# Order of the gather rows and the count words in the preparation of a graph-network kernel

## The chip, the cores and the metric

The kernel runs on one core of a Trainium2 chip. The metric is the device time of one execution in microseconds (us). A core has TensorE (PE; PEld is its weight load), VectorE (DVE), ScalarE (ACT), GpSimd (POOL) and SyncE (SP), which issues most transfers; GpSimd issues the indirect fetches.

## The reference, cut to what matters

The inputs are 12500 nodes with 64 features (`x`), 400000 edges (`src`, `dst`, sorted by `dst`) and 64 attributes for each edge. Three rounds each gather the features of every edge's source node and add them up at its destination:

```python
edge_index = jnp.stack([src, dst])
x = _layernorm(x + _L0_gnn_ref(x, src, dst, L0_gnn_W_fc, L0_gnn_b_fc, L0_gnn_W_res, L0_gnn_b_res), axis=-1)
x = _layernorm(x + _L1_gnn_ref(x, edge_index, edge_attr_64, ...), axis=-1)
# inside: segment_sum(x[src], dst) in L0; segment_sum(x[src] @ Wm + edge_attr @ We, dst) twice in L1
```

## The kernel before, in words

The sums over edges are done in two ways. Most edges are **counted**: for a window of 1, 2 or 4 destination nodes, a matmul of two one-hot matrices counts how many edges come from each source node, and the counts (kept as an adjacency matrix) are multiplied with the features. Edges that no window covers are **gathered**: their source rows are fetched from a table in memory and added with a one-hot matmul. Both ways need codes for every edge, and all codes depend on the data, so the program makes them itself. This is the **preparation**, the first stage of the program; nothing of the main loops starts before the step marked `prepared` (L730). The change touches preparation alone.

The edges form T = 3125 tiles of 128. There are 34 columns (CG) of 128 count steps, so CW = 4352 columns, and 26 columns (SG) of 128 gather steps, SPAD = 3328. The order of the work on each engine is written out by hand; engines meet at semaphores. VectorE numbers most of its instructions on one semaphore (`step`), and other engines wait for a named mark in that count.

VectorE in order: it finds where windows lie among the tiles (`c_tile`, L552); marks the covered edges and packs source, destination and that mark into one word for each edge (`both`, L571), which SP stores to `both_dram` (L1479); counts listed tiles (`sums`, L582). Then, as the kernel stands:

- **Count list** (L585 to L594): GpSimd has fetched 34 columns of `dst` tile rows into `rows_ct` (L1233, L1234); VectorE compares and counts in two halves (L587, L589) and writes the indices `c_idx`.
- **Gather list** (L597 to L649): after two small products of TensorE (L1030, L1031) VectorE finds the tile and the block of every gather step and writes `g_idx` (L646).
- **Edge list and path** (L652 to L665), then two memsets and two instructions on all count columns (L671, L672).
- **x loop** (L674 to L685): with TensorE (L1058) and ScalarE (L1343, L1346) the table of the first round, y, is made in 7 iterations of 14 blocks and stored by SP (L1494).
- **Unpacking of the count words** (L687 to L699): 16 instructions on 4352 columns (two of the steps are four instructions each, one for each window width, `spans_of`), after all 34 fetches into `rows_c` have landed. The codes lie in `accf` (`rel`) and `tmp_c`.
- **Unpacking of the gather rows** (L703 to L714): 6 instructions for each half of 13 columns, when that half of the fetches has landed. They write `src_g` and `rel_g`.
- Two sums of biases, then 14 **copies of the turned gather codes** from PSUM (L724), a wait, and the memset `prepared` (L730).

GpSimd issues the fetches in this order: 34 for `rows_ct`; 34 of count words (`c_idx`, L1237); 26 of gather rows (`g_idx`, L1239, L1240). Then three memsets: most of `abuf[:, 1]` (L1242) after the x loop, the accumulator (L1245) after the marks of L714 and ScalarE's turned codes, and the rest of `abuf[:, 1]` (L1247) after VectorE's copies. All fetches stand on one line, that of the helper `fetch` (L1228).

TensorE turns the codes by transposes of 128 columns, four to a PSUM bank: `prepare` (L1012) for those that ScalarE copies out (L1337, one instruction for each 128 columns; count codes are written twice side by side), `prepare_side` (L1021) for those that VectorE copies out. SP loads x in 14 transfers (L1490) after `c_idx`.

## Time and profile before

| | us |
|---|---|
| median of 3 runs | 3540.97 (3540.76 to 3543.51) |
| the profiled execution | 3540.19 |
| its span, first to last instruction | 3538.4 |
| preparation, until `prepared` | 258.3 |
| busy in the span: PE, DVE, POOL, ACT | 3093.2, 2386.6, 2122.3, 1585.2 |

How to read it: a timeline row gives the start in us from the span's start, the duration, the engine, the line of the kernel, the operation, the tiles written and read with partitions x elements, how many instructions are merged (x5), and in brackets how long the engine sat idle before and what released it. The stage table gives busy time and, in brackets, the number of instructions in each window; PEclk is the granted TensorE clock as a share of full speed. A landing is the time from the start of a DMA's issue until its data are there. Preparation is one chain through several engines: a busy share alone says little there, and what counts is who waits for whom.

### The profile page before, as it was taken

How to read it: one execution, taken by the hardware profiler on the slowest of the kernel's cores; microseconds unless marked ns; L12 is line 12 of the kernel's file. 1: busy time of each engine (PE TensorE's matmuls, PEld its weight loads, DVE VectorE, ACT ScalarE, POOL GpSimd, SP SyncE). 2: the span in 40 equal slices, each digit the busy share in tenths (PEclk: the TensorE clock that was granted, in tenths of full speed). 3: DMA queues.
4: the chain of work that ended last, by engine and by line, in shares of the span. 5: the costliest groups of instructions: out<-in, count | busy, mean ns of one | idle time of the engine just before them, and what ended most of it. 6: DMA issues, size and time to landing. Idle time of an engine off the chain costs nothing.

```text
span 3538.4 us, 114817 instructions
## 1 busy us (share of the span) xinstructions
PE 3093.2 (87%) x38568; PEld 2873.9 (81%) x38568; DVE 2386.6 (67%) x6286; ACT 1585.2 (45%) x2164; POOL 2122.3 (60%) x2436
## 2 busy tenths in 40 slices
PE   0228999999999999889999979999999889999995
PEld 0127988888888888778888879999999789999995
DVE  8679998988888888689999673333333433333335
ACT  0122677778999999689999550000000400000000
POOL 5771345455666666444444257777777777777774
PEclk9869999999999999999999879999999999999998
DMA  3521455555666666578888439999999499999995
GB/s 86 145 18 44 162 200 203 201 219 223 242 242 242 242 242 242 216 225 253 253 252 253 131 117 386 393 396 383 400 391 385 176 358 398 387 388 398 383 394 222
DMA packets 234014, 928.09 MB, mean 262 GB/s; under 512 B 46723, under 2 KB 146193, under 8 KB 178030
## 3 DMA queue, kind: packets, MB, share of 16 engines
q1 hardware_dynamic: 182559, 846.33, 63.9%
q0 software_dynamic: 51392, 80.97, 8.0%
q8 instruction: 34, 0.56, 0.1%
q14 instruction: 29, 0.24, 0.0%
HBM read 676.56 MB, written 250.56 MB: 262 GB/s over the span
## 4 chain that ended last, share of the span: by engine, by line
PE 40%; POOL 18%; issue 17%; DVE 13%; DMA 6%; DVEq 5%; ACT 1%; ACTq 0%; POOLq 0%; SPq 0%
PE ps L1124 28%; POOL msg L1286 13%; PE ps L1147 8%; DVE union L815 5%; DMA msg<-y_tab,idx 4%; POOL abuf L1228 3%; DVE union L929 3%; PE ps L1116 3%; DVE abuf L942 2%; DVEq L942 2%; DVEq L470 2%; POOL union L1228 1%; PE ps L1084 1%; DMA abuf<-in_x_dram 1%; PE ps L1203 1%
## 5 line engine op out<-in xcount | busy, mean ns | idle before, releaser
L1286 POOL DMA_INDIRECT msg<-y_tab,idx x1512 | 1612.8, 1067 | 920.1 <-issue 469.3
L1124 PE MATMUL ps<-union,abuf 128*128 128x192 bf16 x14112 | 1205.8, 248 | 15.9 <-DVEq L786 10.2
L1124 PEld LDWEIGHTS ps<-union,abuf 128*128 128x128 f16 x14112 | 1173.2, 99 | 18.9 <-issue 10.6
L1416 ACT ACTIVATE abuf<-ps 128x784 f16<-128x784 f32 x1152 | 949.1, 824 | 261.7 <-PE ps L1147 236.9
L815 DVE TENSOR_TENSOR union<-lane,union 128x1568 f16<-128x1568 f16 (+1 forms) x1384 | 912.2, 711 | 8.2 <-PE ps L1147 4.9
L1124 PE MATMUL ps<-early,abuf 128*128 128x195 bf16 x7154 | 809.3, 249 | 0.0
L1124 PEld LDWEIGHTS ps<-early,abuf 128*128 128x128 f16 x7154 | 641.9, 99 | 92.1
L1147 PE MATMUL ps<-union 128*128 128x98 f16 (+2 forms) x4192 | 661.3, 287 | 56.9 <-DVE union L815 55.9
L1392 ACT ACTIVATE idx<-src_g 128x7 int32 (+1 forms) x216 | 44.4, 206 | 1255.8 <-PE ps L1116 1228.1
L807 DVE TENSOR_TENSOR acc<-acc,ps 128x64 f32 (+1 forms) x1015 | 225.3, 222 | 409.4 <-DVE acc L807 239.6
L1194 PE MATMUL ps<-union 128*64 128x128 f32 x7280 | 458.5, 278 | 24.2 <-ACT union L1434 19.6
L1194 PEld LDWEIGHTS ps<-union 128*64 128x64 f32 x7280 | 395.4, 137 | 87.5 <-DVE abuf L942 75.6
L1434 ACT ACTIVATE union<-union 128x1280 f32<-128x1280 f16 x364 | 443.6, 1268 | 35.7 <-DVE union L929 35.3
L1147 PEld LDWEIGHTS ps<-union 128*128 128x128 f16 x4192 | 353.2, 108 | 98.5 <-issue 58.8
L1306 POOL TENSOR_TENSOR rel_e<-early,base_e 128x10 f16 x728 | 225.7, 329 | 261.1 <-DVE union L929 244.8
L929 DVE TENSOR_TENSOR union<-lane,rel_e 128x640 f16<-128x640 f16 x728 | 353.6, 486 | 4.4 <-POOL rel_e L1306 1.4
L890 DVE TENSOR_REDUCE part_d<-ps 128x64 f32<-128x192 f32 x144 | 51.6, 359 | 356.9 <-PE ps L1124 356.9
L793 DVE TENSOR_SCALAR hot_g<-lane,codes 128x128 f16<-128x128 f16 x1008 | 182.4, 272 | 63.6 <-DVE acc L807 62.1
L1116 PE MATMUL ps<-msg,hot_g 128*128 128x64 bf16 (+1 forms) x4536 | 182.2, 195 | 43.5 <-DMA msg<-y_tab,idx 43.2
L942 DVE TENSOR_TENSOR abuf<-abuf,ps 128x128 f32 x728 | 206.2, 283 | 15.4 <-issue 7.2
L1116 PEld LDWEIGHTS ps<-msg,hot_g 128*128 128x128 f16 x4536 | 169.4, 99 | 52.9 <-DMA msg<-y_tab,idx 52.0
L864 DVE TENSOR_TENSOR acc<-acc,ps 128x65 f32 x504 | 110.6, 219 | 69.0 <-DVE acc L864 53.8
(231 smaller groups left out, 1342.2 us busy)
## 6 DMA issues: line engine op xcount, KB each, us to landing
abuf<-a_dram SPq DMA_DIRECT2D x288, 1568.0 KB
a_dram<-abuf SPq DMA_DIRECT2D x72, 3136.0 KB
union<-in_edge_attr_dram SPq DMA_DIRECT2D x728, 160.0 KB, 3.1
msg<-y_tab,idx POOLq DMA_INDIRECT x1512
y_tab<-union SPq DMA_DIRECT2D x28, 336.0 KB, 2.2
abuf<-in_x_dram SPq DMA_DIRECT2D x28, 224.0 KB, 3.7
y_tab<-early SPq DMA_DIRECT2D x7, 682.5 KB, 5.6
out_dram<-union SPq DMA_DIRECT2D x2, 800.0 KB, 3.5
```

The costliest lines, as they stand in the source:

```text
L807: V.tensor_tensor(to, to, tile_ps(r, j, k).unsqueeze(1), ALU.add).then_inc(s_add[r], 1)
L815: return V.tensor_tensor(to.rearrange("p s (c u) -> p s c u", u=2), lanes.unsqueeze(1).to_broadcast([P, n, width // 2, 2]), codes[:, which ...
L929: marks = V.tensor_tensor(mark_e[:, h, :, :].rearrange("p j (c u) -> p j c u", u=2), lane16[:, 0:P].rearrange("p (c u) -> p c u", u=2).uns ...
L942: V.tensor_tensor(to, to, ps[:, b, 0:P], ALU.add).then_inc(e_add, 1)
L1116: last = nc.tensor.matmul(tile_ps(r, j, k), hot_g[:, s, :], msg[:, s, c * width_of[r]:(c + 1) * width_of[r]], start=c == 0, stop=c == 2)
L1124: last = nc.tensor.matmul(ps[:, bank, 0:3 * width_of[r]], abuf[:, buffer, hi * P:(hi + 1) * P], ycols[r][:, hi, :], start=hi == 0, stop=hi ...
L1147: nc.tensor.matmul(ps[:, w % 4, 0:WIN].rearrange("p (h d) -> p h d", d=WD)[:, :, d0:d0 + wd], hot_c[:, n, WIN:WIN + P], hot_c[:, n, 0:HIS ...
L1194: last = nc.tensor.matmul(ps[half:half + D, h, 0:P], feats[:, h, j * D:(j + 1) * D], hot_e[:, h, j, :], start=j < 2, stop=j >= EG - 2)
L1286: pool.indirect_dma_start(msg[:, s, 0:3 * width_of[r]], None, y_tab[r], bass.IndirectOffsetOnAxis(ap=idx[:, s:s + 1], axis=0)).then_inc(ga ...
L1306: nc.gpsimd.tensor_tensor(rel_e[:, h, :, :], flat(dst_e[:, bass.ds(grp[h], 1), :]).unsqueeze(2) .to_broadcast([P, EG, 2]), base_e[:, bass. ...
L1416: A.activation(abuf[:, j, :].rearrange("p (h w d) -> p w h d", w=WPB, d=WD) [:, w:w + 2, :, :], ps[:, w % 4:w % 4 + 2, 0:WIN].rearrange("p ...
L1434: A.activation(hot_e[:, h:h + 2, :, :], mark_e[:, h:h + 2, :, :], ACT.Copy)\
```

## The change

The gather list moves ahead of the count list on VectorE, and the fetches of gather rows ahead of those of the count words on GpSimd. The first half of the gather rows is unpacked before the x loop, the second after it. The count words are fetched and unpacked in two halves, 16 and 18 columns (`C_HALF` = 16). ScalarE copies out the gather codes and the first half of the count codes, and of the second half the one table (`twice_h`); VectorE copies the other (`twice_l`), 5 groups. ScalarE now copies a whole group of 512 columns by one instruction. `rel` moves from `accf` to a part of `abuf` (`rel_cf`), and the memsets change accordingly. Cut to its core (the function `unpack_g` holds the six instructions of L706 to L714 as they were; of the count list and the unpacking of count words, moved or cut to column ranges, only the heads stand here):

```diff
+    C_HALF = BC // 2 * 4
+    BL = BC - BC // 2
+    BP = 1 + 2 * BG + 2 * BC - BL
...
+        rel_cf = af[:, 2 * SPAD:2 * SPAD + CW]
...
             step(V.tensor_tensor_scan(upto[:, 0:TC], node[:, 0:TC], spans[:, 0:TC], 0.0, ALU.mult, ALU.add), "sums")
-            for c0, c1, landed in ((0, CG // 2, s_g[2]), (CG // 2, CG, s_late)):
...
-            step(V.tensor_copy(gidx[:, 2, :], small[:, 18, :]), "c_idx")
...
             step(V.scalar_tensor_tensor(base_n, blk_n, float(P), past_n, ALU.mult, ALU.add))
+            for c0, c1, landed in ((0, CG // 2, s_g[2]), (CG // 2, CG, s_late)):
...
+            step(V.tensor_copy(gidx[:, 2, :], small[:, 18, :]), "c_idx")
...
-            rel, tmp = accf[:, 0:CW], tmp_c
+            rel, tmp = rel_cf, tmp_c
...
+            unpack_g(0, SG // 2, s_g[0])
             for i in range(XITER + 1):
...
-            dve.wait_ge(s_g[1], 16 * CG)
...
+            unpack_g(SG // 2, SG, s_last)
+            for c0, c1, landed, upto, name in ((0, C_HALF, s_g[1], 16 * C_HALF, "code_0"),
+                                               (C_HALF, CG, s_late, 16 * (CG - CG // 2 + CG - C_HALF), "code_1")):
+                dve.wait_ge(landed, upto)
...
-            for to, first in ((code_g, 0), (src_g, BG)):
-                for n in range(first, first + BG):
-                    dve.wait_ge(s_ptd, n + 1)
-                    g0 = (n - first) * 4
-                    width = min(4, SG - g0) * P
-                    V.tensor_copy(to[:, g0 * P:g0 * P + width], ps[:, 4 + n % 4, 0:width]).then_inc(s_pd, 1)
-            dve.wait_ge(s_pd, 2 * BG)
+            for n in range(BL):
+                dve.wait_ge(s_ptd, n + 1)
+                cols = slice(C_HALF * P + n * 4 * P, min(C_HALF * P + (n + 1) * 4 * P, CW))
+                width = cols.stop - cols.start
+                V.tensor_copy(twice_l[:, cols, :], ps[:, 4 + n % 4, 0:width].unsqueeze(2).to_broadcast([P, width, 2]))\
+                    .then_inc(s_pd, 1)
+            dve.wait_ge(s_pd, BL)
+            dve.wait_ge(s_pc, BP)
...
-            prepare(0, 1 + BC)
...
+            prepare(0, BP - BL)
+            pe.wait_ge(x_left, XITER)
+            for n in range(BL):
+                prepare(BP - BL + n, BP - BL + n + 1)
+                prepare_side(n)
...
-            pool.wait_ge(s_v, mark["c_idx"])
+            pool.wait_ge(s_v, mark["g_idx"])
             pool.wait_ge(s_both, 32)
-            fetch(rows_c, single(both_dram), 2, range(CG), s_g[1])
-            pool.wait_ge(s_v, mark["g_idx"])
             fetch(rows_g, tiles_of(both_dram), 0, range(SG // 2), s_g[0])
             fetch(rows_g, tiles_of(both_dram), 0, range(SG // 2, SG), s_last)
-            LEFT = 2 * (2 * SPAD) - HIS * P
+            pool.wait_ge(s_v, mark["c_idx"])
+            fetch(rows_c, single(both_dram), 2, range(C_HALF), s_g[1])
+            fetch(rows_c, single(both_dram), 2, range(C_HALF, CG), s_late)
+            LEFT, RIGHT = 2 * (2 * SPAD) - HIS * P, 2 * (2 * SPAD + CW) - HIS * P
             pool.wait_ge(x_low, XITER)
-            pool.memset(abuf[:, 1, LEFT:], 0.0).then_inc(s_clear, 1)
-            pool.wait_ge(s_pc, 1 + BC)
-            pool.wait_ge(s_v, mark["src_g"])
+            pool.memset(abuf[:, 1, RIGHT:], 0.0).then_inc(s_clear, 1)
+            pool.wait_ge(s_pc, 1 + 2 * BG)
+            pool.memset(abuf[:, 1, 0:LEFT], 0.0).then_inc(s_clear, 1)
+            pool.wait_ge(s_v, mark["rel_g"])
             pool.memset(acc_all[:, :, :], 0.0).then_inc(s_clear, 1)
-            pool.wait_ge(s_pd, 2 * BG)
-            pool.memset(abuf[:, 1, 0:LEFT], 0.0).then_inc(s_clear, 1)
...
+                    elif jobs[n][2] is not None:
+                        to = jobs[n][2]
+                        frm = ps[:, n % 4, 0:to.shape[1]]
+                        if len(to.shape) == 3:
+                            frm = frm.unsqueeze(2).to_broadcast(list(to.shape))
+                        last = A.activation(to, frm, ACT.Copy)
```

## Rows read from the trace of the kernel before

**Rows 1.** Stages: window, length, busy us of PE, PEld, DVE, ACT, POOL, PEclk

```profile
0.00:258.50 258.50, 38.48 (x289) 35.56 (x289) 195.35 (x208) 33.72 (x86) 176.15 (x109) 0.83 0.39 85
...
142.20:160.20 18.00, 10.50 (x71) 9.78 (x71) 14.94 (x15) 11.24 (x15) 14.10 (x13) 0.83 0.86 279
...
167.30:204.50 37.20, 0.02 (x1) 0.03 (x1) 36.55 (x16) 0.00 (x0) 33.84 (x12) 0.50 0.27 30
...
207.20:215.30 8.10, 5.49 (x35) 4.17 (x33) 7.89 (x6) 8.10 (x32) 7.34 (x3) 0.91 0.30 30
```

**Rows 2.** Timeline of GpSimd: start, duration, line, operation, idle time before it

```profile
114.31 0.94 POOL L1228 DMA_INDIRECT union<-both_dram,gidx  x1 [8.04 <-DVE tiles L598]
...
138.54 4.51 POOL L1228 DMA_INDIRECT union<-both_dram,gidx  x1 [0.30 <-issue]
...
199.92 4.62 POOL L1228 DMA_INDIRECT abuf<-both_dram,gidx  x1 [0.31 <-issue]
...
224.44 0.94 POOL L1228 DMA_INDIRECT abuf<-both_dram,gidx  x1 [0.30 <-issue]
...
225.37 9.94 POOL L1242 MEMSET abuf<- 128x11776 f16 x1
...
239.29 6.39 POOL L1245 MEMSET acc<- 128x6500 f32 x1 [3.99 <-DVE abuf L709]
```

**Rows 3.** Timeline of VectorE in preparation, same columns

```profile
108.26 2.42 DVE L587 TENSOR_TENSOR abuf<-abuf,sc 128x2176 f32<-128x2176 int32 x1 [12.84 <-DMA abuf<-in_dst_dram,gidx]
...
114.07 0.16 DVE L598 COPY tiles<-ps 125x1 f32<-125x1 f32 x1
...
131.32 0.18 DVE L646 CAST gidx<-small 128x26 int32<-128x26 f32 x1
...
137.55 4.69 DVE L672 TENSOR_TENSOR union<-lanef,small 128x4352 f32<-128x4352 f32 x1
...
167.36 2.43 DVE L688 TENSOR_SCALAR union<-union 128x4352 int32<-128x4352 int32 x1 [7.22 <-DMA union<-both_dram,gidx]
...
202.00 2.43 DVE L699 CAST union<-union 128x4352 f32<-128x4352 int32 x1
...
214.25 1.03 DVE L714 TENSOR_SCALAR abuf<-abuf 128x1664 f32<-128x1664 f32 x1
...
231.37 4.82 DVE L706 TENSOR_SCALAR acc<-abuf 128x1664 int32<-128x1664 int32 x1 [16.09 <-DMA abuf<-both_dram,gidx]
...
242.20 4.37 DVE L714 TENSOR_SCALAR abuf<-abuf 128x1664 f32<-128x1664 f32 x1
...
247.84 1.48 DVE L724 CAST code_g<-ps 128x512 f16<-128x512 f32 x2 [0.50 <-PE ps L1021]
...
250.05 2.93 DVE L724 CAST code_g<-ps 128x512 f16<-128x512 f32 x5 [0.73 <-PE ps L1021]
...
258.27 0.17 DVE L730 MEMSET part_d<- 128x130 f32 x1 [0.99 <-POOL abuf L1247]
```

**Rows 4.** Groups of instructions: GpSimd's gather-row fetches (165 to 225.5 us)

```profile
L1228 POOL DMA_INDIRECT abuf<-both_dram,gidx x26 | 52.5, 2019 | 7.9 <-issue 7.9
```

**Rows 5.** Timelines of TensorE and ScalarE in preparation, same columns

```profile
91.01 0.57 PE L1031 MATMUL ps<-tiles,hot_g 125*128 125x1 f32 x2
...
246.62 1.97 PE L1021 MATMUL ps<-ident,abuf 128*128 128x128 f32 x8 [31.26 <-DVE abuf L714]
...
250.92 5.48 ACT L1337 ACTIVATE union<-ps 128x256 f16<-128x256 f32 x18 [0.23 <-PE ps L1012]
```

**Rows 6.** DMA issues: median us from issue to landing (125 to 140; 224 to 226 us)

```profile
union<-both_dram,gidx POOLq DMA_INDIRECT x12, 2.6
...
abuf<-both_dram,gidx POOLq DMA_INDIRECT x2, 6.8
```

**Rows 7.** Stage table, first steps of the main loop (columns as in rows 1)

```profile
262.00:266.00 4.00, 3.73 (x23) 3.35 (x24) 3.41 (x7) 0.00 (x0) 3.14 (x3) 0.50 0.20 37
...
280.00:290.00 10.00, 8.47 (x90) 6.87 (x88) 10.00 (x20) 1.65 (x2) 0.00 (x0) 1.00 0.01 2
```

More of the change, by code:

```diff
@@ L649, in _ @@
             step(V.scalar_tensor_tensor(base_n, blk_n, float(P), past_n, ALU.mult, ALU.add))
+            for c0, c1, landed in ((0, CG // 2, s_g[2]), (CG // 2, CG, s_late)):
+                dve.wait_ge(landed, 16 * (c1 - c0))
+                step(V.tensor_tensor(by_step(before_ct)[:, c0:c1, :], by_step(rows_ct)[:, c0:c1, :],
+                                     over(sc[:, 0, c0:c1], c1 - c0), ALU.is_lt))
+                step(V.tensor_reduce(small[:, 16, c0:c1], by_step(before_ct)[:, c0:c1, :], AX.X, ALU.add))
+            step(V.scalar_tensor_tensor(small[:, 17, :], small[:, 6, :], float(P), small[:, 16, :],
+                                        ALU.mult, ALU.add))
+            step(V.tensor_tensor(small[:, 17, :], small[:, 17, :], sc[:, 1, :], ALU.add))
+            step(V.tensor_scalar(small[:, 18, :], small[:, 17, :], float(E - P), None, ALU.min))
+            step(V.tensor_copy(gidx[:, 2, :], small[:, 18, :]), "c_idx")
             e_left, e_grp, e_blk, e_base, e_hit = (small[:, k, 0:ES] for k in (2, 3, 4, 5, 12))
@@ L673, in _, with unpack_g @@
                                  over(small[:, 3, :], CG), ALU.is_lt))
+            lane_bits = P.bit_length() - 1
+            def unpack_g(c0, c1, landed):
+                dve.wait_ge(landed, 16 * (c1 - c0))
+                n, cols = c1 - c0, slice(c0 * P, c1 * P)
+                step(V.tensor_single_scalar(lane_of[:, 0:n * P], rows_g[:, cols], P - 1, op=ALU.bitwise_and))
+                step(V.tensor_scalar(block_of[:, cols], rows_g[:, cols], lane_bits, P - 1,
+                                     ALU.logical_shift_right, ALU.bitwise_and))
+                step(V.scalar_tensor_tensor(src_gf[:, cols], lane_of[:, 0:n * P], float(BLOCKS), block_of[:, cols],
+                                            ALU.mult, ALU.add), "src_g")
+                step(V.tensor_single_scalar(rows_g[:, cols], rows_g[:, cols], BITS, op=ALU.logical_shift_right))
+                step(V.tensor_tensor(by_step(rel_gf[:, cols]), by_step(rows_g[:, cols]), over(base_n[:, c0:c1], n),
+                                     ALU.subtract))
+                step(V.tensor_scalar(rel_gf[:, cols], rel_gf[:, cols], -1.0, float(P), ALU.max, ALU.min), "rel_g")
+            unpack_g(0, SG // 2, s_g[0])
             for i in range(XITER + 1):
@@ L685, in _ @@
                                     yparts[0][:, x_blocks(i - 1), 1, 0:D], ALU.subtract).then_inc(x_low, 1)
-            dve.wait_ge(s_g[1], 16 * CG)
-            step(V.tensor_scalar(dst_c, rows_c, BITS, WIDE - 1, ALU.logical_shift_right, ALU.bitwise_and))
-            step(V.tensor_tensor(by_step(rel), by_step(dst_c), over(sc[:, 0, :], CG), ALU.subtract))
-            for s0, s1, wd in spans_of:
-                step(V.scalar_tensor_tensor(tmp[:, s0:s1], rel[:, s0:s1], float(wd), tmp[:, s0:s1], ALU.is_ge, ALU.add))
@@ L980, in _ @@
                         V.tensor_tensor(squares[:, blk, :], feat[:, blk, :], over_d(rstd[:, blk]), ALU.mult).then_inc(f_scaled, 1)
[L983 to L989 removed]
+        jobs = [(mark["path"], [(regs, 64, P, trT)], None)]
+        for into, frm, name, to, first, cols in ((jobs, rel_gf, "rel_g", code_g, 0, SG), (jobs, src_gf, "rel_g", src_g, 0, SG),
+                                                 (jobs, rel_cf, "code_0", twice_h, 0, C_HALF), (jobs, tmp_c, "code_0", twice_l, 0, C_HALF),
+                                                 (jobs, rel_cf, "code_1", twice_h, C_HALF, CG), (side_jobs, tmp_c, "code_1", twice_l, C_HALF, CG)):
+            for g0 in range(first, cols, 4):
+                g1 = min(g0 + 4, cols)
+                into.append((mark[name], [(frm[:, g * P:(g + 1) * P], P, P, None) for g in range(g0, g1)],
+                             to[:, g0 * P:g1 * P, ...]))
+        assert len(side_jobs) == BL and len(jobs) == BP
         e_src = dst_rows.rearrange("p (a q j) -> p a j q", a=TC // EG, j=EG)
@@ L1060, in _ @@
                 last.then_inc(x_prod, 1)
-            prepare(0, 1 + BC)
-            side = 0
-            for n in range(1 + BC, 1 + 2 * BC):
-                prepare(n, n + 1)
-                while side < 2 * BG and (side < 2 * (n - BC - 2) or n == 2 * BC):
-                    prepare_side(side)
-                    side += 1
+            prepare(0, BP - BL)
[3 more added lines that the diff above has]
+                prepare_side(n)
             for r in range(3):
```

65 lines of the change are left out of this document (20 added, 45 removed).

## The prediction, made before the changed kernel ran

> **What bounds the kernel now.** I read the stage table first, because every edit lies before the first product of the main loops. Preparation ends at 258.5 us, and VectorE is busy for 195 of them, GpSimd for 176 [rows 1]. The chain of waits then names GpSimd's gather fetches for most of this stage, so I followed VectorE's and GpSimd's timelines side by side. The reader is to see three things in them.
>
> First, GpSimd has one queue of 94 fetches, about 1.24 us apart when nothing is in their way (0.94 plus 0.30 of issue), and the last ends at 225.38 [rows 2]. It stands idle for 8.04 us between 106.26 and 114.31, while VectorE in turn waits 12.84 us for the last rows of the second search [rows 2, 3].
>
> Second, the fetches lengthen beside certain VectorE work. The 26 gather-row fetches take 52.5 us of execution plus 7.9 of issue, against 32.2 at the free pace [rows 4]. One lasts 4.51 us and ends 0.81 after L672, which reads two SBUF tensors, has ended (142.24); another lasts 4.62, past the start of L699's cast (202.00), and ends 0.11 after that has ended (204.43) [rows 2, 3]. So a fetch that meets a two-input instruction must wait for its end to begin, and beside the doubled-rate single-input ones it is held a second time before it can finish. Beside the unpacking of the count words (167.36 to 204.43) twelve fetches fill a stretch of 37.2 us [rows 1]; 14.9 would do.
>
> The Trainium skill ("SBUF — State Buffer", the section on the shared port pair) infers that a tensor_tensor leaves descriptor generation alone. The L672 row disagrees: 4.51 against 0.94. I follow the row; the rule is a rival below.
>
> Third, a GpSimd memset does the reverse: VectorE's L706 takes 4.82 us and L714 4.37, against 1.03 for another L714 of the same size, and both end 0.9 us after a memset does [rows 2, 3]. Behind the last landing come the unpacking of the second half of gather rows, TensorE's turning of them, 14 VectorE copies, and the reset that lets all engines go at 258.27 [rows 3].
>
> **The change part by part.**
>
> *The gather list goes first.* The list needs TensorE's two small products (91.58) [rows 5] and then 17.4 us of VectorE (114.07 to 131.50) [rows 3]: it is ready at 109.1. GpSimd's search fetches lose the company of one two-input instruction of 2.42 us (about 1.6 us less) and gain that of the list's (about 3): they end near 107.7. GpSimd's idle time falls from 8.04 to some 1.7, and the first gather fetch starts at 109.4. The count list now comes behind: four instructions of 2.42 and four small ones put it at 120.5, 6.6 later than now, but its fetches wait for 26 others anyway. Queued behind the same mark on SP are 14 loads of x, also 6.6 later; VectorE wants the products of the first only at 144, so that costs nothing; if the loads took all of the 23 us from 120.5, it would still be covered.
>
> *26 gather fetches.* 32.2 us free. What they meet: the two L587 (about 1.6 and 1.2 lost), L672 (3.4), the unpacking of their own first half (about 3.5), and a stretch of the x loop (1.2). Together 10.9, so GpSimd is done with them at 152.5. The first 13 are issued by 131.4. They land 2.6 to 6.8 us after their start, by the fast and the slow row [rows 6]; I take 136, since the loads of x run beside. VectorE is then held at that wait from 130.5, with the x loop queued behind it: 8.1 us of unpacking to 144, 18.0 of x loop to 162, 8.1 for the other half to 170 [rows 1]. The next thing for VectorE comes only at 181.7, so up to 11 us of delay here is covered.
>
> *16 count fetches.* 19.8 free, about 3.3 lost to the x loop and 4.6 to the second unpacking (as the three fetches beside that work lose now): issued by 180.1, landed by 181.7.
>
> *First half of the count words.* The 16 instructions now take 37.1 us. With 0.195 us of each fixed (0.16 from the two sizes 1.03 at 1664 and 2.43 at 4352 columns, and the gap) there are 33.9 us by size. 2048 of 4352 columns in 14 instructions cost 16.0 + 2.7 = 18.7: 181.8 to 200.5.
>
> *18 count fetches beside it.* Free 22.3. The loss is the term the trace doesn't show. Bounds: nothing, or the 0.60 us per us that the full-size instructions cost now (22.3 over 37.2), 11.2 over 18.7. Walking the fetches past the shorter instructions by the two rules above lets eight through in the stretch and loses 9.4; I take that, near the upper end because the same kinds of instruction stand there. The queue ends at 211.8; the last fetch starts at 210.9 and, landing like the lone count fetches (2.6), is in at 213.5.
>
> *Memsets.* GpSimd goes straight from the last fetch to its first memset, 3072 columns, 2.6 us at L1242's rate [rows 2], to 214.5. VectorE's first instruction of the second half is a doubled-rate one and waits for that: 0.9 lost (between nothing and the 9.6 of all three memsets: 11776 columns take 9.94 now, the accumulator's 6.39). The 6.4 us memset of the accumulator should follow beside two-input instructions, which do not wait for a memset now.
>
> *Second half of the count words.* 2304 columns in 12 instructions: 18.0 + 2.3 = 20.3, to 234.8. This used to be hidden behind the gather fetches; now the gather rows are hidden and this lies on the path.
>
> *The tail.* The 14 VectorE copies of gather codes (about 0.6 each, 8.4 us) go to ScalarE between 170 and 181, where it is idle now: nothing. Left are ten groups, five on each engine. VectorE's first copy stands 1.27 us after the unpacking now; one group of four transposes comes ahead of it, about 1.0 (eight take 1.97) [rows 3, 5]. Four copies of 1.14 (0.59 plus 512 more elements at 1.08 ns, L672's rate) and a short one of 0.65 make 5.2. With 0.15 until the reset: 7.6 us. ScalarE's five, at four times 0.304 each [rows 5], end by 6.8. The reset comes at 242.4 instead of 258.27.
>
> *Sum.* The queue's end moves by 13.6 us (8.04 - 1.7 = 6.3 of idle time, 7.3 of less holding), the way from there by 2.3 (32.9 to 30.6): 15.9. The profiled execution took 3540.19 with a span of 3538.4, 0.78 under the median, so 3524.3 on its scale and **3525.0** as a median. All later stages are unchanged and only begin earlier. A measurement of this kernel can tell about 0.2%, 7 us, from no change.
>
> **The rivals.**
>
> *Late landing meets the memset* (0.17). The last lone gather fetches land 6.8 us after their start, not 2.6 [rows 6]. If the last count fetches do so, the data come at 217.7, in the middle of the accumulator's memset (215.1 to 221.5), and the first instruction waits as L714 does now. From 221.5: 20.4 and 7.6 give 249.5, a gain of 8.8: 3532. Against it: twelve count fetches in a row landed in 2.6. It decides if the data come after 215.1.
>
> *Little holding* (0.10). If the fetches slip through between the halved instructions, up to 9.4 us more are won: 3516 to 3520.
>
> *Two-input instructions hold no fetch* (0.03). Then the gather and count fetches lose only what five doubled-rate instructions per half cost, the queue ends near 191, and the reset comes near 221: 3504. The 4.51 us row speaks against it. This is what the Trainium skill's inference (same page and section) would make of it.
>
> *The clock of the first steps* (0.03), the slower side. TensorE starts the main loop at the lower of its two levels (1.2 GHz): 0.50 from 262 to 266 with 23 products in 4 us; later it is at 1.00 with 90 in 10 [rows 7]. It has fewer transposes to do just ahead. Each us at the low level loses 1 - 5.75/9.0 = 0.36 us; the gain is gone after 44 us of it, and twice that would cost 32: 3557. Against it: it starts low now as well, and the whole of preparation has work for TensorE in 38 of 258 us either way [rows 1].
>
> *The reset is not what the main loop waits for, or the lists do not come early* (0.05): 3541. Nothing in the trace supports it: VectorE waits for nothing but the last memset there, and the main loop's first instructions follow the reset [rows 3].
>
> **How the numbers follow.** The forecast has 0.62, with its own range of 3520 to 3530 (holding 5 to 11.2, landing 2.4 to 4). The range reaches over the late landing and part of the little holding: 3517 to 3533. Faster by over 0.2% (below 3533.9): 0.62 + 0.17 + 0.10 + 0.03, less 0.03 for a worse mix, 0.89; within: 0.07; slower: 0.04.
>
> **What would show it.** The first gather fetch near 109.4; fetch 26 ending near 152.5; first-half gather wait on VectorE until about 136; an idle stretch on VectorE from 170 to 182; about eight fetches between 182 and 200; the last issue near 212; the first instruction of the second half lengthened by under 1 us; the reset near 242. It is wrong if the queue ends outside 204 to 215, or if the step from the last landing to the reset is not near 29 us.

## The result, and the profile after

The change made the kernel slower, by a third of a per cent. In eight runs of each the kernel before took 3541.44 us (median; 3539.79 to 3543.63) and the changed kernel 3552.64 us (3550.02 to 3555.53): a ratio of 1.0033, 95% interval 1.0024 to 1.0042. The forecast was 3525.0 us with a range of 3517 to 3533. The profiled execution of the changed kernel took 3550.02 us with a span of 3548.3, so it compares with the profiled 3540.19 (span 3538.4) of before.

Preparation did win. The time came back more than a thousand microseconds later, in two stages that the change doesn't touch: the **edge loop** (VectorE marks edges one-hot, TensorE multiplies, VectorE adds the products up; 728 steps, 32 to a turn of VectorE's loop) and the **fold** behind it (196 fp32 products of 128 x 64 columns). From the starts of four rows in each trace (the resetting memset, the loop's first marks, the fold's first product and the end):

| stretch | before, us | after, us | difference |
|---|---|---|---|
| start to `prepared` | 258.27 | 246.35 | -11.9 |
| `prepared` to the edge loop's first marks | 1252.71 | 1251.86 | -0.9 |
| edge loop, first marks to fold | 478.68 | 482.76 | +4.1 |
| fold | 22.10 | 40.60 | +18.5 |
| end of the fold to the end of the span | 1526.64 | 1526.73 | +0.1 |

The resets and the folds stand further down and in [rows 3]; the first marks, of before and of after:

```profile
1510.98 0.49 DVE L929 TENSOR_TENSOR union<-lane,rel_e 128x640 f16<-128x640 f16 x1 [1.40 <-POOL rel_e L1306]
```

```profile
1498.21 0.49 DVE L940 TENSOR_TENSOR union<-lane,rel_e 128x640 f16<-128x640 f16 x1 [1.40 <-POOL rel_e L1317]
```

**Preparation.** The stage table of the changed kernel, columns as in [rows 1]: all of preparation, the x loop, the unpacking of the first half of the count words, and the first steps of the main loop.

```profile
0.00:246.50 246.50, 42.12 (x289) 39.89 (x289) 193.55 (x209) 33.25 (x45) 158.05 (x109) 0.83 0.41 89
148.00:171.50 23.50, 12.35 (x71) 11.41 (x71) 14.73 (x14) 11.23 (x15) 18.12 (x18) 0.72 0.93 209
179.60:198.30 18.70, 7.91 (x52) 7.67 (x52) 18.23 (x14) 6.97 (x14) 16.26 (x9) 0.68 0.31 49
...
250.00:254.00 4.00, 3.65 (x22) 3.27 (x23) 3.40 (x7) 0.00 (x0) 3.08 (x4) 0.50 0.18 37
```

VectorE's work is nearly the same, GpSimd's is 18 us less; the x loop takes 23.5 us instead of 18.0, for the same work [rows 1]. The main loop starts at the same low clock, with one product fewer in 4 us [rows 7]. The timeline of GpSimd, columns as in [rows 2]:

```profile
109.44 0.94 POOL L1239 DMA_INDIRECT abuf<-both_dram,gidx  x1 [2.27 <-DVE small L639]
...
127.11 4.51 POOL L1239 DMA_INDIRECT abuf<-both_dram,gidx  x1 [0.31 <-issue]
...
150.90 1.14 POOL L1239 DMA_INDIRECT abuf<-both_dram,gidx  x1 [0.30 <-issue]
...
208.68 0.94 POOL L1239 DMA_INDIRECT union<-both_dram,gidx  x1 [0.30 <-issue]
209.62 2.68 POOL L1254 MEMSET abuf<- 128x3072 f16 x1
212.22 0.76 POOL L1256 MEMSET abuf<- 128x768 f16 x1
212.89 5.53 POOL L1258 MEMSET acc<- 128x6500 f32 x1
```

These are the first, the 13th and the 26th gather fetch, the last count fetch and the three memsets behind it. The idle time ahead of the first gather fetch has shrunk from 8.04 to 2.27 us, and the queue ends at 209.62 instead of 225.38 [rows 2]. The same on VectorE, columns as in [rows 3]:

```profile
126.11 4.69 DVE L676 TENSOR_TENSOR union<-lanef,small 128x4352 f32<-128x4352 f32 x1
139.92 1.03 DVE L684 TENSOR_SCALAR acc<-abuf 128x1664 int32<-128x1664 int32 x1 [9.11 <-DMA abuf<-both_dram,gidx]
...
168.39 1.09 DVE L700 TENSOR_TENSOR abuf<-ps,early 128x896 f32<-128x896 f32 x1 [6.03 <-ACT early L1357]
...
179.61 1.23 DVE L713 TENSOR_SCALAR union<-union 128x2048 int32<-128x2048 int32 x1
...
211.60 8.04 DVE L713 TENSOR_SCALAR union<-union 128x2304 int32<-128x2304 int32 x1 [13.32 <-DMA union<-both_dram,gidx]
219.68 2.56 DVE L714 TENSOR_TENSOR abuf<-union,sc 128x2304 f32<-128x2304 int32 x1
...
237.21 1.36 DVE L724 CAST union<-union 128x2304 f32<-128x2304 int32 x1
...
246.35 0.17 DVE L741 MEMSET part_d<- 128x130 f32 x1
```

Two rows need a second look. L713 of the second half takes 8.04 us; another single-input instruction of the same size, the cast L724, takes 1.36. It ends at 219.64, which is 1.22 us after the last of GpSimd's three memsets has ended (212.89 + 5.53 = 218.42): it was kept out through all three. And the x loop stands still for 6.03 us at 162, because TensorE waits for x; this one is covered.

**Fold.** The timelines of TensorE, first of the kernel before and then of the changed one:

```profile
1981.92 6.47 PE L1194 MATMUL ps<-union 128*64 128x128 f32 x100 [0.34 <-DVE abuf L942]
1989.66 22.10 PE L1203 MATMUL ps<-twofold,abuf 128*128 128x64 f32 x196 [1.27 <-DVE abuf L953]
```

```profile
1973.23 6.48 PE L1205 MATMUL ps<-union 128*64 128x128 f32 x100 [0.38 <-DVE abuf L953]
1980.97 40.60 PE L1214 MATMUL ps<-twofold,abuf 128*128 128x64 f32 x196 [1.26 <-DVE abuf L964]
```

The stage tables of the fold tell why, again of before and then of after:

```profile
1990.00:1995.00 5.00, 5.00 (x47) 5.00 (x46) 0.69 (x1) 1.19 (x2) 0.00 (x0) 1.00 0.01 3
```

```profile
1980.00:1985.00 5.00, 4.03 (x26) 4.03 (x27) 1.57 (x4) 0.60 (x1) 0.00 (x0) 0.76 0.01 3
1985.00:1990.00 5.00, 5.00 (x25) 5.00 (x25) 0.00 (x0) 0.60 (x1) 0.00 (x0) 0.50 0.00 0
```

The granted clock is 1.00 (2.4 GHz) before and 0.50 (1.2 GHz) after: 47 products in 5 us against 25. A mean of 0.76 from 1980 to 1985 is 2.6 us at the full clock, so it falls at 1982.6, 1.6 us after the fold has begun. TensorE worked at the full clock until then but for a pause of 1.26 us in front of the fold, where it waits for VectorE's last additions. The kernel before has the same pause, 1.27 us, and keeps its clock.

**Edge loop.** Short waits of VectorE ahead of its additions, in the view of waits over the loop (line waited at, releaser, us in total, times, longest; "issue": nothing that the profile shows), of before and then of after:

```profile
DVE abuf L942 <- issue: 7.2, 25, 0.3
```

```profile
DVE abuf L953 <- issue: 14.5, 66, 0.4
```

In the timeline they come once per turn of the loop before and three times after. A turn takes 20.74 us before and 20.97 after:

```profile
1576.23 0.29 DVE L942 TENSOR_TENSOR abuf<-abuf,ps 128x128 f32 x1 [0.29 <-issue]
...
1596.97 0.29 DVE L942 TENSOR_TENSOR abuf<-abuf,ps 128x128 f32 x1 [0.29 <-issue]
```

```profile
1557.75 0.29 DVE L953 TENSOR_TENSOR abuf<-abuf,ps 128x128 f32 x1 [0.15 <-issue]
...
1563.28 0.29 DVE L953 TENSOR_TENSOR abuf<-abuf,ps 128x128 f32 x1 [0.29 <-issue]
...
1565.94 0.29 DVE L953 TENSOR_TENSOR abuf<-abuf,ps 128x128 f32 x1 [0.17 <-issue]
...
1578.72 0.29 DVE L953 TENSOR_TENSOR abuf<-abuf,ps 128x128 f32 x1 [0.15 <-issue]
```

### The profile page after: what moved, and what is told of

Its sections match the earlier page's. It is cut to its first block, busy times and chain, and to the rows that moved or that the text cites. A ratio compares the mean times of both kernels' runs of the same rounds, so it can differ in the third digit from the quotient of the medians.

```text
span 3548.3 us, 114777 instructions
## 1 busy us (share of the span) xinstructions
PE 3114.4 (88%) x38568; PEld 2894.7 (82%) x38568; DVE 2383.8 (67%) x6287; ACT 1584.4 (45%) x2123; POOL 2101.3 (59%) x2436
## 4 chain that ended last, share of the span: by engine, by line
PE 35%; issue 19%; POOL 17%; DVE 16%; DMA 6%; DVEq 5%; ACT 1%; POOLq 0%; SPq 0%; ACTq 0%
PE ps L1135 23%; POOL msg L1297 15%; PE ps L1158 7%; DVE union L826 5%; DMA msg<-y_tab,idx 4%; DVE union L940 3%; PE ps L1127 2%; DVE abuf L953 2%; DVEq L953 2%; DVEq L474 2%; PE ps L1214 1%; DMA abuf<-in_x_dram 1%; DVE union L570 1%; PE ps L1095 1%; POOL abuf L1281 0%
## 5 line engine op out<-in xcount | busy, mean ns | idle before, releaser
L953 DVE TENSOR_TENSOR abuf<-abuf,ps 128x128 f32 x728 | 204.8, 281 | 20.3 <-issue 14.5
```

The source lines that it names most:

```text
L953: V.tensor_tensor(to, to, ps[:, b, 0:P], ALU.add).then_inc(e_add, 1)
```

## The experiments

The first theory was that the loss hangs on *when* the edge loop runs (the shift; theory A of the first expectations, where theory B is that something else in the changed kernel holds the clock down). The second was that it hangs on *where* the loop lies in VectorE's program (the place). e1 to e8 are one execution each, beside one of the kernel before; the others are medians of 4 to 12. In two expectations (e6, e8) the change is said to add some ten VectorE instructions ahead of the loop; counted in the compiled programs it adds one (1120 before, 1121 after: the two sums of biases). Where a short wait count is given below, it is that of the additions from first marks to fold, as shown above; expectations that say 64 counted over a window a little shorter.

### Is it the shift? e1_pad12 and e2_pad2

```diff
+            for _ in range(7):
+                step(V.memset(hot_g[:, :, :], 0.0))
+            step(V.memset(hot_g[:, 0:10, :], 0.0))
             step(V.memset(part_d[:, :, :], 0.0), "prepared")
```

> The changed kernel with eight extra VectorE memsets (about 12 us) just ahead of the reset, which give back what preparation won and do nothing else. Theory A (the level of TensorE's clock in the fold hangs on when the fold begins, because the 1.3 us pause ahead of it can bring the lower level): the 196 fold products may return to about 22 us, and the time is then near 3546 (3552.6 + 12 - 18.5). Theory B (something the change left behind, not the shift, holds the clock low): the fold stays at 40.6 us and the time is near 3564.

3564.91 us, the reset at 254.08 (7.7 us later than in the changed kernel, not the 12 of the expectation), the fold still slow:

```profile
1993.14 39.74 PE L1217 MATMUL ps<-twofold,abuf 128*128 128x64 f32 x196 [1.26 <-DVE abuf L967]
```

e2 adds one full memset and one of three columns (1.9 us, two instructions).

> The changed kernel with about 1.9 us of extra VectorE memsets ahead of the reset. Theory A: the fold can come out either way, 22 or 40.6 us, with a time near 3536 or 3554.5; a 22 here would show that 2 us of shift are enough to change the clock. Theory B: 40.6 us, near 3554.5.

3553.38 us, the fold 40.34 us, 66 short waits. Two delays, and the fold slow at each: starting later gives nothing back. Both pads also add VectorE instructions ahead of the loop, eight and two; that this matters came out only with e5 and e6.

### Is it the pause ahead of the fold? e3_fill

```diff
+                    pe.wait_ge(e_add, ESTEPS + EB)
+                    for n in range(16):
+                        nc.tensor.matmul(ps[0:D, 0, 0:P], feats[:, 0, 0:D], hot_e[:, 0, 0, :], start=True, stop=True)
                     pe.wait_ge(e_add, ESTEPS + LAG + EB)
                     for n in range(FOLDS):
```

> The changed kernel with 16 dummy products of the edge loop's shape between the last edge product and the fold, written to a PSUM bank that the fold overwrites: TensorE's pause of 1.26 us goes, nothing else moves. Theory A (the pause brings the low level): granted clock 1.00 over the fold, fold 22 us, time near 3534. Theory B (the fold's products cannot hold the clock after this change whatever comes ahead): fold 40.6, time unchanged near 3552.6.

3541.55 us, 11 under the changed kernel; 3534 was forecast. Against the profiled execution of the changed kernel the edge loop with the added products took 2.8 us more, and the stretch behind the fold 6.4, which no run explains. TensorE's timeline has no pause in front of the fold, and the fold runs at the full clock:

```profile
1980.99 3.66 PE L1211 MATMUL ps<-union 128*64 128x128 f32 x32
1984.58 22.10 PE L1217 MATMUL ps<-twofold,abuf 128*128 128x64 f32 x196
```

The pause is needed for the fall. It doesn't bring it about alone, since the kernel before has it too. VectorE's short waits (62) stay as in the changed kernel, and the loop stays long (485.6 us with the added products in it).

### What did the memsets cost? e4_dve_memsets

The three memsets go to VectorE, into its idle time ahead of the second half of the count words; GpSimd's are removed.

```diff
+                if c0:
+                    dve.wait_ge(x_low, XITER)
+                    step(V.memset(acc_all[:, :, :], 0.0))
+                    step(V.memset(abuf[:, 1, RIGHT:], 0.0))
+                    dve.wait_ge(s_pc, 1 + 2 * BG)
+                    step(V.memset(abuf[:, 1, 0:LEFT], 0.0))
                 dve.wait_ge(landed, upto)
```

> The changed kernel with GpSimd's three memsets moved to VectorE, into its idle stretch ahead of the second half of the count words. If the memsets held VectorE's first instruction of that half (8.04 us against 1.36), it now takes 1.4 and the reset comes 5.5 to 6.7 us earlier, near 240; if that instruction was slow for another reason, it stays at 8 and nothing moves. The memsets may slow fetches beside them by up to 3 us. The total is not forecast beyond this: theory A lets the fold come out at 22 or 40.6, so 3527 or 3546; theory B says 3546.

3547.76 us. In VectorE's timeline the first instruction of the second half takes 1.36 us and the reset comes 6.7 us earlier; the fold took 40.16 us again.

```profile
199.34 5.47 DVE L713 MEMSET acc<- 128x6500 f32 x1 [1.42 <-issue]
...
211.28 1.36 DVE L720 TENSOR_SCALAR union<-union 128x2304 int32<-128x2304 int32 x1 [4.22 <-DMA union<-both_dram,gidx]
...
239.66 0.17 DVE L747 MEMSET part_d<- 128x130 f32 x1
```

So the held instruction cost what the row says, 8.04 - 1.36 = 6.7 us.

### Does the kernel before lose it too? e5_before_pad2, e6_before_tiny10, e15_before_tiny1, e10_before_gpsimd_pad

e5 is the kernel before with the two memsets of e2 ahead of the reset; e6 and e15 put ten and one memsets of a single element into an early wait of VectorE:

```diff
+            for _ in range(10):
+                step(V.memset(part_d[0:1, 0, 0:1], 0.0))
             dve.wait_ge(stored[0], 16)
```

> The kernel before with about 1.9 us of extra VectorE memsets ahead of the reset, nothing else. Theory A (the fold's clock hangs on where its pause falls in time, and the kernel before is lucky): the fold may fall to the low level, about 40 us instead of 22.1, and the time is then near 3561; if it stays at 22 the time is near 3543. Theory B (the changed preparation itself is the cause): 22 us and 3543 for certain.

> The kernel before with ten one-element memsets on VectorE early in preparation, where it waits for a load anyway: no step of preparation moves, but VectorE's later instructions lie ten places further on, as in the changed kernel. If the edge loop's extra waits of the changed kernel (64 short ones called issue against 25) come from where VectorE's instructions lie: about 64 waits and an edge loop (first marks to fold) 3 to 5 us longer than 478.7. If they come from anything else: 25 waits and 478.7. The fold comes out at 22 or 40 under theory A, at 22 under theory B.

e5 took 3565.90 us and e6 3567.86, against 3540.83 of the kernel before beside them. Nothing of the change is in either, and both show the whole loss. Of e5, the timeline of TensorE and the view of waits:

```profile
1995.92 39.68 PE L1206 MATMUL ps<-twofold,abuf 128*128 128x64 f32 x196 [1.26 <-DVE abuf L956]
```

```profile
DVE abuf L945 <- issue: 14.9, 68, 0.4
```

e6 speaks against the shift: its ten instructions lie in an idle wait, and its reset comes at 259.59, 1.3 us later than before.

e10 is the counterpart: the delay without a VectorE instruction, by three more memsets on GpSimd that VectorE's wait ahead of the reset includes.

```diff
+            pool.wait_ge(s_clear, 2)
+            for n in range(3):
+                pool.memset(abuf[:, 1, 0:LEFT], 0.0).then_inc(s_clear, 1)
+                pool.wait_ge(s_clear, 3 + n)
             pool.memset(abuf[:, 1, 0:LEFT], 0.0).then_inc(s_clear, 1)
```

> The kernel before with three further GpSimd memsets of 0.8 us each ahead of the resetting memset, each behind the last: the later stages begin some 2.4 us later, as in the padded kernel before with two instructions on VectorE, but VectorE's program has no instruction more. The place of the edge loop: 25 short waits, the edge loop 478.7 us, the fold 22.1 us, the program 3542 to 3545 us. The shift in time: the fold 40 us, the program 3560 to 3566 us.

3543.58 us (ratio 1.0009, 0.9993 to 1.0024), with one of ten executions at 3560.80. The reset comes at 261.38, later than in e5 and e6, and there are 25 short waits and a fast fold, as the place has it and the shift does not:

```profile
1991.16 22.10 PE L1203 MATMUL ps<-twofold,abuf 128*128 128x64 f32 x196 [1.24 <-DVE abuf L953]
```

> The kernel before with one one-element memset on VectorE in an early wait. A place that a single instruction reaches: 60 to 67 short waits, the edge loop 483 us, the fold 22 or 40 us, the program 3544 or 3562 us. A boundary that lies further (two instructions reached it in e5): 25 waits, 478.7 us, 3541 us.

3542.39 us (ratio 1.0002, 0.9987 to 1.0018), with one of ten executions at 3559.65; in the profile 25 short waits, the fold 22.10. One instruction more does nothing to the kernel before; two do.

### Is it chance? e7_after_again

The changed kernel, unaltered.

> The changed kernel once more, unaltered, for another trace. Theory A with a chance phase in every run: the fold comes out at 22 in some runs. If it is 40 again, with the clock falling at another distance from the pause, the outcome belongs to the program more than to chance. Time near 3552.6.

3555.64 us, the fold 40.58 us, 64 short waits: the same again.

### Undo the one instruction: e9_after_one_sum

```diff
-            for c in range(2):
-                step(V.tensor_tensor(bme[:, c, 0, :], bme[:, c, 0, :], bme[:, c, 1, :], ALU.add))
+            step(V.tensor_tensor(bme[:, :, 0, :], bme[:, :, 0, :], bme[:, :, 1, :], ALU.add))
```

> The changed kernel with its two sums of the biases written as one instruction over both codes, as in the kernel before: VectorE's program then has as many instructions ahead of the edge loop as before the change (the changed kernel has one more). Nothing else moves. The place of the edge loop in VectorE's program: the short waits of VectorE in the edge loop number about 25 as before (64 in the changed kernel), the edge loop from its first marks to the fold takes 478.7 us (482.8), the fold's 196 products take 22.1 us at the full clock (40.6), and the program takes 3541.4 - 11.9 = 3529.5 us (3526 to 3532). The rival, that the shift in time of the edge loop decides (it begins 12 us earlier than before): 62 to 67 waits or not, the fold takes 40 us and the program 3549 to 3556 us.

3529.74 us as a median of twelve, forecast 3529.5; ratio to before 0.9963 (0.9947 to 0.9978). The whole change of preparation is in it, and the reset comes at 247.77. The timeline of TensorE and the view of waits:

```profile
1977.88 22.10 PE L1213 MATMUL ps<-twofold,abuf 128*128 128x64 f32 x196 [1.26 <-DVE abuf L963]
```

```profile
DVE abuf L952 <- issue: 7.4, 26, 0.3
```

The edge loop takes 478.63 us, as before. One instruction decides over some 23 us (3552.64 - 3529.74). One of the twelve executions took 3547.06 us, 17 above the median, about the fold's price; it has no profile.

### A version that beats both, and what a place is: e8, e11 to e14, e16 to e18

e8 joins e3 and e4 and adds 54 one-element memsets, to move the loop on in VectorE's program.

> The changed kernel with the dummy products ahead of the fold, the three memsets on VectorE, and 54 one-element VectorE memsets early in preparation (where it waits for a load), which with the change's ten put VectorE's later instructions 64 places on. Dummy products: fold 22, so about 16 us less than 3552.6 (18.5 less 2.3 of their own). Memsets: about 6.5 less. Together 3530. If 64 places bring the edge loop back to 25 waits, another 4 less: 3526; if not, 3530.

3529.41 us, with a fast fold (the filling products) and an edge loop of 484.32 us, as long as ever: 46 waits at the additions and 21 at the marks. Moving on by 58 instructions did not bring the short loop back.

e11 goes the other way: e4 and e9 together, and three memsets of the start moved to GpSimd, so that VectorE has 1120 instructions ahead of the loop, as in the kernel before. e12 is e11 with e3's filling products.

```diff
-            V.memset(steps[0:1, 0:GW + SETS * GW + EDGE0], 0).then_inc(s_zero, 1)
-            V.memset(w_cat[:, :, :, :], 0.0).then_inc(s_zero, 1)
-            V.memset(w_y0[:, :, :], 0.0).then_inc(s_zero, 1)
...
+            pool.memset(w_cat[:, :, :, :], 0.0).then_inc(s_zero, 1)
+            pool.memset(w_y0[:, :, :], 0.0).then_inc(s_zero, 1)
+            pool.memset(steps[0:1, 0:GW + SETS * GW + EDGE0], 0).then_inc(s_zero, 1)
```

> The changed kernel with the three memsets on VectorE's idle stretch instead of GpSimd, the sums of the biases as one instruction, and three memsets of the start on GpSimd, so that VectorE's program again has as many instructions ahead of the edge loop as before the change. The place of the edge loop: 25 short waits, the edge loop 478.7 us, the fold 22.1 us, resetting memset at 240, the program 3541.4 - 11.9 - 6.6 = 3523 us (3519 to 3527). The shift in time: the fold 40 us, the program 3542 to 3548 us.

> The same with 16 products whose result nobody reads between the last edge product and the fold. The fold takes 22.1 us under both theories. The place of the edge loop: 25 short waits, the edge loop with the added products 481 us, the program 3523 + 2.4 = 3525.5 us (3521 to 3529), slower than without them by 2.4 us. The shift in time: 62 to 67 waits and an edge loop of 485 us, the program 3529 us, faster than without them by 15 us.

Neither theory had e11 right: 68 short waits in spite of the equal count, a loop of 482.63 us, and in the profiled execution a fast fold (3523.38 us). Its ten executions fall into two groups, four from 3523 to 3530 us and six from 3543 to 3552; the median of 3544.06 (ratio 0.9997, 0.9978 to 1.0015) lies in the upper one. That the groups are the fold at its two clocks is inferred from their distance, since no execution of the upper one was profiled. e12, where TensorE doesn't pause, has no such groups, though it is slower than both theories said (3525.5 and 3529): 3531.22 to 3533.66, median 3532.21, ratio 0.9968 (0.9954 to 0.9983).

e13 drops one of e11's waits that earlier instructions imply. The expectation counts it as a second semaphore of the accumulator's memset; in the built program it is an instruction of its own ahead of that memset. e14 is e13 with the filling products.

```diff
-                    dve.wait_ge(x_low, XITER)
                     step(V.memset(acc_all[:, :, :], 0.0))
```

> e11_best_plain without VectorE's wait on the x products ahead of the moved memsets, which its earlier copies imply: the same instructions, one instruction with two semaphores fewer. If a second semaphore takes a place in VectorE's program: some 25 short waits instead of 65, the edge loop 478.7 us instead of 482.6, the program 3519 to 3524 us wherever the fold runs at the full clock (22.1 us). If it takes none: 65 waits and an edge loop of 482.6 us as in e11.

> The same with 16 products whose result nobody reads between the last edge product and the fold. If a second semaphore takes a place: some 25 short waits, the edge loop from first marks to the fold 478.7 + 2.4 = 481.1 us, the fold 22.1 us in every run, the program 3532 (e12) - 4 = 3528 us. If it takes none: 65 waits and 3532 us as e12.

Both missed: 61 short waits, a loop of 482.94 us. e13 again falls into two groups (four of twelve at 3527 to 3528, eight from 3544 to 3549; median 3544.54, ratio 0.9994, 0.9976 to 1.0012), e14 does not (median 3530.57, ratio 0.9958, 0.9942 to 0.9974).

e16 and e17 then take one and two further instructions off VectorE's program ahead of the loop; e18 is e17 with the filling products.

```diff
-            step(V.memset(dsts[0:1, 0:HALO], -1000))
...
-            step(V.memset(ones_t, 1.0))
...
+            pool.memset(sums[0:TP, TP:TP + P], 1.0).then_inc(s_const, 1)
+            pool.memset(dsts[0:1, 0:HALO], -1000).then_inc(s_const, 1)
```

> e13 with one memset of the start moved from VectorE to GpSimd, so that VectorE has one instruction fewer ahead of the edge loop than the kernel before. The place in VectorE's program: 22 to 26 short waits, the edge loop 478.7 us, the fold mostly 22.1 us, the median 3520 us. Something else: 59 to 65 waits, the edge loop 482.5 us, the median 3526 or 3544 us as the fold falls.

> e13 with two memsets of the start moved to GpSimd. The place: 22 to 26 short waits, the edge loop 478.7 us, the median 3520 us. Something else: 59 to 65 waits, 3526 or 3544 us.

> e17 with the 16 products ahead of the fold: the fold 22.1 us in every run. The place: 25 waits and 3526 to 3528 us, some 3 us less than e14's 3530.6. Something else: 3530 to 3533 us.

As the place has it: e16 3520.68 us (ratio 0.9948, 0.9931 to 0.9964), **e17 3520.44 us** (0.9943, 0.9926 to 0.9959), e18 3524.72 us (0.9958, 0.9941 to 0.9975), a little under its forecast of 3526 to 3528. e16 and e17 are the fastest of all and can't be told apart. With the short loop the filling products cost: e18's four executions (3522 to 3527) all lie above e17's (3518 to 3522). The view of waits and the two rows of its timelines:

```profile
DVE abuf L952 <- issue: 7.0, 24, 0.3
```

```profile
240.73 0.17 DVE L740 MEMSET part_d<- 128x130 f32 x1
...
1970.57 22.10 PE L1213 MATMUL ps<-twofold,abuf 128*128 128x64 f32 x196 [1.27 <-DVE abuf L963]
```

All kernels in the order of their place. A place is counted here as one for each VectorE instruction ahead of the loop and one for each further semaphore that such an instruction waits on, in the compiled program:

| kernel | instructions | places | all VectorE instructions | short waits | edge loop, us |
|---|---|---|---|---|---|
| e17, e18 (filled) | 1118 | 1158 | 1188 | 24, 24 | 477.7, 479.4 |
| before, e10 | 1120 | 1158 | 1188 | 25, 25 | 478.7, 479.1 |
| e16 | 1119 | 1159 | 1189 | 24 | 477.6 |
| e15 | 1121 | 1159 | 1189 | 25 | 478.7 |
| e9 | 1120 | 1160 | 1189 | 26 | 478.6 |
| e13, e14 (filled) | 1120 | 1160 | 1190 | 61, 61 | 482.9, 485.8 |
| e5 | 1122 | 1160 | 1190 | 68 | 483.7 |
| after, e7, e3 (filled) | 1121 | 1161 | 1190 | 66, 64, 62 | 482.8, 482.7, 485.6 |
| e11, e12 (filled) | 1120 | 1161 | 1191 | 68, 68 | 482.6, 485.9 |
| e2 | 1123 | 1163 | 1192 | 66 | 483.2 |
| e4 | 1124 | 1165 | 1195 | 69 | 484.3 |
| e6 | 1130 | 1168 | 1198 | 68 | 483.1 |
| e1 | 1129 | 1169 | 1198 | 68 | 484.4 |
| e8 (filled) | 1178 | 1219 | 1249 | 46, and 21 at the marks | 484.3 |

Up to 1159 places the loop is short, from 1161 on it is long, over changes that have nothing else in common; 1160 stands on both sides, and so does 1120 among the instructions. The fourth column sorts all twenty exactly: it counts every VectorE instruction of the built program ahead of the loop, register and branch instructions too, and a wait that stands by itself as one, however many semaphores it names. Up to 1189 the loop is short, from 1190 on long. By this count e11 has three instructions more than the kernel before, which fits its long loop.

What is shown: a loop with 1190 VectorE instructions ahead of it, instead of 1189, has three short waits a turn instead of one and takes 4 us more. The two added waits stand ahead of a turn's additions 4 and 24 (counted from 0), 128 instructions apart. In e8, 59 instructions further on than the changed kernel, the wait at addition 24 is gone and one at addition 16 stands at about the same instruction of the program (1359; 1351 to 1359 in the others). This fits waits at fixed places in the program; e8's other wait, at its first marks, has no such counterpart.

What VectorE does in these waits stays open: the profile names no releaser for them. That it waits for a part of its program to come from memory is not what the traces show: the view of DMA has 34 and 29 packets on two queues of instructions over the whole span, but for some 450 us of the edge loop, long or short, not one in any of the twenty profiles (changed kernel: none from 1516.6 to 1971.5 us).

The Trainium skill ("Advanced Engine Details and Errata", section "ISA Cache") gives an engine's store for its program as two lines of 256 instructions each. The traces don't bear out that one more border of such lines in the loop is the whole cause: its body of 207 instructions can hold at most one, and the step adds two waits a turn. No run here shows the size of such a line.

## Why the prediction was wrong

**The step that failed** is the sentence behind the sum, "All later stages are unchanged and only begin earlier". Their code was unchanged and their time was not: +4.1 us in the edge loop and +18.5 in the fold, together 22.6 of the 25.7 us by which the profiled execution (3550.02) missed the forecast on its scale (3524.3). With the one instruction taken back, e9, the same preparation gives 3529.7, faster than before, inside the range of 3517 to 3533.

The chain from the change to the loss, as far as the runs go: one VectorE instruction more (e9 takes it away, and the loss with it) puts the edge loop past a place in VectorE's program (the table); each turn then takes 0.2 us more; and behind the longer loop TensorE's pause of 1.26 us ahead of the fold mostly ends with the clock falling, which it doesn't where the pause is filled (e3). Of nine profiles with the long loop and the pause, seven have a fold of 39.7 to 40.6 us and two (e11, e13) one of 22.1; all six with the short loop and the pause have 22.1, and so have the five without the pause (e3, e8, e12, e14, e18).

**What stays open** is what VectorE waits for in the long loop, and why the same pause costs the clock mostly behind the long loop and seldom behind the short one: that link is a count of profiles, not a mechanism. The kernel before isn't safe either: of 69 runs of it beside e9 to e18, eight took 3555 to 3563 us, 14 to 22 above their median, though none of these was profiled.

**Preparation, by the steps of the forecast.** It ended at 246.35, not 242.4.

- *Gather list first*: right. First gather fetch at 109.44 (forecast 109.4), after 2.27 us of idle time.
- *26 gather fetches*: done at 152.04 (152.5). They took 35.0 us of execution beside shorter work, against 52.5 [rows 4], and the count fetches 47.2:

```profile
L1239 POOL DMA_INDIRECT union<-both_dram,gidx x34 | 47.2, 1389 | 10.4 <-issue 10.4
L1239 POOL DMA_INDIRECT abuf<-both_dram,gidx x26 | 35.0, 1346 | 9.9 <-issue 7.6 <-DVE small L639 2.3
```

- *Landing of the first 13*: the 13th fetch ended at 131.62, as forecast (131.4), but VectorE waited until 139.92, not 136. The view of DMA issues from 126 to 132 us has the loads of x and the fetches beside each other, both slow to land; [rows 6] had 2.6 and 6.8:

```profile
abuf<-in_x_dram SPq DMA_DIRECT2D x3, 224.0 KB, 12.9
abuf<-both_dram,gidx POOLq DMA_INDIRECT x3, 9.9
```

- *x loop and second half of the gather rows*: done at 179.58, not 170, with 6.03 us of waiting for x in it. The forecast said that up to 11 us of delay here is covered, and the count words' first half indeed started in place, at 179.61, with the idle stretch of 170 to 182 used up.
- *First half of the count words*: 18.7 us, as forecast. Eight fetches got through beside it, as forecast.
- *End of the queue*: 209.62 (211.8); the last data landed 2.9 us after their fetch began, at 211.60 (213.5).
- *Memsets*: **the mis-sized term**. Forecast 0.9 us, measured 6.7 (e4 takes it away). The forecast had VectorE's instruction enter behind the first memset. It entered behind the third: between three memsets that follow each other without a gap it found no room. The upper bound of the term, 9.6, held this case; the value was taken from the wrong end.
- *Second half and tail*: from the end of L713 to the last unpacking row 18.9 us and 7.8 from there to the reset; forecast 18.9 (20.3 less the first instruction's 1.4) and 7.6.

So 2 us were won more than forecast at the queue's end and 5.8 lost at the memsets: 4.0 us of the miss.

**The rivals.** *Late landing meets the memset* had the right mechanism and about the right price under the wrong condition: the data came at 211.60, before the 215.1 from which it was to decide, and the instruction was held all the same. *Two-input instructions hold no fetch* is out: beside L676, which reads two SBUF tensors, a fetch takes 4.51 us again, as in [rows 2]. *The clock of the first steps* named the right resource in the wrong place: the main loop's first 4 us have 22 products at 0.50, against 23 before [rows 7]; what lost its clock was the fold, 1730 us later. *Little holding* is out: the queue ended 2.2 us earlier than forecast, not up to 9.4. *The reset is not what the main loop waits for* is out too: the way from `prepared` to the first marks changed by 0.9 us. No rival had a mechanism in which an added instruction moves the code behind it.

The Trainium skill ("SBUF — State Buffer", section "SBUF: two separate sides") says of the port pair that VectorE and GpSimd share that whoever has it keeps it for a whole instruction while the other is fully blocked. The trace agrees and adds that three instructions in a row keep it as one: 8.04 us instead of 1.36.

## What to carry to other kernels

Compare the untouched stages of the two traces first: a change at the start can move a loop behind it to another place in an engine's program, and here one added instruction cost 23 us, twice what the change had won. Where a loss can't be traced to an edit, add or take away one instruction in an idle wait and see whether it stays. A short pause of TensorE ahead of a long run of products is worth filling where the clock falls behind it and stays down (e11 and e13 have 14 of 22 executions in the upper group, e12 and e14 none), but the filling has its own price, some 4 us here (e18 against e17). And GpSimd's memsets don't belong next to a single-input VectorE instruction on the path.

## What was not expected of the hardware

- Behind a pause of 1.26 us TensorE's clock fell from 2.4 to 1.2 GHz, 1.6 us into the fold, and stayed there for the other 39 us although TensorE was busy for 5.00 of every 5 us (the fold's stage table). The fold took 40.6 us instead of 22.1. With the pause filled it took 22.1 in all five profiles (e3, e8, e12, e14, e18); the kernel before has the pause and kept its clock in its profile.
- One-element memsets in an idle wait of VectorE cost the kernel 27 us if there are ten of them (e6, one execution: 3567.86 against 3540.83) and nothing if there is one (e15: 3542.39 against 3541.45).
- A VectorE instruction that had to wait for a GpSimd memset waited for the two that followed it directly as well: 8.04 us instead of 1.36.
